# Mixed order in the last group of the attention sums, and four low parts of the first weights on GpSimd

## The chip, the cores and the metric

The kernel runs on one core of a Trainium2 chip. The metric is the device time of one execution in microseconds. Before the change the median of three runs was 1007.03 us (1006.68 to 1008.79).

## What is computed

Four graph layers over 1250 nodes with 1024 features, each with a layer norm and a relu ahead of it and added to its input:

```python
h = jnp.maximum(_layernorm(x), 0.0)
x = x + _L0_gnn_ref(h, ...)   # x1 = h @ W1 + b1 (512 columns), then four gated sums over a fixed graph
h = jnp.maximum(_layernorm(x), 0.0)
x = x + _L1_gnn_ref(h, ...)   # h @ W.T + bias, W scattered from the edges and their weights
h = jnp.maximum(_layernorm(x), 0.0)
x = x + _L2_gnn_ref(h, ...)   # graph convolution
h = jnp.maximum(_layernorm(x), 0.0)
x = x + _L3_gnn_ref(h, ...)   # graph attention

# inside _L3_gnn_ref
e = jnp.exp(-jax.nn.leaky_relu(al[src] + ar[dst], negative_slope=NEG_SLOPE))
rowsum = jax.ops.segment_sum(e, src, num_segments=N)
h_prime = jax.ops.segment_sum(e[:, None] * h[dst], src, num_segments=N)
return jax.nn.elu(h_prime / (rowsum[:, None] + EPS))
```

Two places matter here: the product with `W1` at the very start, and the weighted sums `h_prime` at the very end.

## The kernel before

The nodes lie in T = 10 tiles of 128 rows. Every float32 matrix product is made of three passes with the split of a value into a high part (rounded to the type that TensorE takes) and a low part (what is left): high by high, high by low, low by high. ScalarE writes the high parts with a copy, VectorE the low parts with a subtraction. All engines' programs are written out by hand and run in their written order; semaphores tie them together.

**The start.** `w1_raw` comes in four DMAs as KT = 8 pieces of 128x512. ScalarE writes `w1_hi[k]` (L1015) and counts `w_hi_ready`; VectorE writes `w1_lo[k]` = `w1_raw[k]` - `w1_hi[k]` for all eight (L1400) and counts `w_lo_ready`. Then VectorE goes on with the statistics of the third tile (L495 to L499), the choice of each window's edges (`here` L1297, `edges` L1300), `hT_lo` of the second tile (L553), the names of the cells (`src_i` L1305, `node` L1306 and on), and after more of the same the first groups of cells (`right` and `left`, L1340 to L1352), which TensorE sums (L1812, L1815) from its third tile on. TensorE's product of a tile (`x1_pe`, L1885 to L1887) takes three matmuls per piece; in the first tile each piece waits for `w_lo_ready`:

```python
if t == 0:
    pe.wait_ge(w_lo_ready, k + 1)
```

TensorE also transposes each next tile (L563), which ScalarE copies as `hT_hi` (L546). GpSimd's queue at that time: constants, the parts of the edge weights (L829 to L837, done by 14 us), then the storing of count rows (L841). Dense layers 1 and 3 count on with the same `w_lo_ready` in `product_pe`.

**The end.** The attention sums go over GROUPS = 5 groups of GRP = 2 tiles of nodes. A step s of a group takes the attention values between tile s and the group's 256 nodes: VectorE (L1672 to L1683), ScalarE (L1204, L1209) and GpSimd (`e_part`, L929) make `att_hi[s]` and `att_lo[s]`, and TensorE (`gat_step`, L2042) adds three products per tile j and half n of the 1024 columns into PSUM: six matmuls per tile j. `row_sums(j)` (L2049) then sums the attention values and counts `gat_ready`; ScalarE reads sums and row sums (L1218, L1219) and counts `gat_read`; VectorE and ScalarE finish the tile (L1692 to L1708, L1224, L1225), and SP stores it. In the first four groups TensorE takes both tiles j at each step. The last group is written out apart: all ten steps for tile 0, its row sums, ten steps for tile 1's first half, its row sums, ten steps for tile 1's second half:

```python
pe.wait_ge(gat_read, T - GRP - 1)
for s in range(T):
    pe.wait_ge(att_lo_ready, T * (GROUPS - 1) + s + 1)
    gat_step(s, 0, range(2))
row_sums(0).then_inc(gat_ready, 1)
pe.wait_ge(gat_read, T - GRP)
for s in range(T):
    gat_step(s, 1, [0])
row_sums(1).then_inc(gat_ready, 1)
for s in range(T):
    last = gat_step(s, 1, [1])
```

Of the kernel before, what the change touches and what calls it, by code (L numbers as in the profile page):

```python
# [14 lines left out]
ALU = mybir.AluOpType  # L15
ACT = mybir.ActivationFunctionType
AX_X = mybir.AxisListType.X
F32 = mybir.dt.float32
# [12 lines left out]
T = -(-N // P)  # L31
NP = T * P
KT = D // P
# [23 lines left out]
GRP = 2  # L57
# [2 lines left out]
SLOTS = 5  # L60
TANH_LEAD = 3
AL_FIRST = T - 2
LAST_SUMS = (2, 3, 4, 0, 1)
EARLY = 3
LN_STEPS = 3
NORM_STEPS = 4
EPS_LN = 1e-5
# [6 lines left out]
def build_program(nc, x, src, dst, edge_weight, w1, b1, gate_w, gate_b, bias1, w2, b2, w3, att, out):  # L74
# [22 lines left out]
    def sem(name):  # L97
        return ctx.enter_context(nc.semaphore(name))
# [20 lines left out]
    w1_raw = at("w1_raw", [P, KT, HID], F32, R_Y + 64 * KIB)  # L119
    w1_hi = at("w1_hi", [P, KT, HID], F32R, R_Y + 24 * KIB)  # L120
# [171 lines left out]
    w_landed = sems("w_landed", 4)  # L292
    w_hi_ready = sem("w_hi_ready")
    w_lo_ready = sem("w_lo_ready")
    copy_landed = sem("copy_landed")
    first_stored = sem("first_stored")
    bias_placed = sem("bias_placed")
# [178 lines left out]
    def split_act(act, d, ks):  # L476

        for k in ks:
            if k % 2 == 0:
                act.wait_ge(w_landed[k // 2], 16 * (d.n + 1))  # L480
            nc.scalar.activation(W_HI[d.n][:, k, :], W_RAW[d.n][:, k, :], ACT.Copy).then_inc(w_hi_ready, 1)

    def split_dve(dve, d, ks):

        for k in ks:
            dve.wait_ge(w_hi_ready, KT * d.n + k + 1)
            nc.vector.tensor_tensor(W_LO[d.n][:, k, :], W_RAW[d.n][:, k, :], W_HI[d.n][:, k, :].bitcast(F32),
                                    ALU.subtract).then_inc(w_lo_ready, 1)
# [77 lines left out]
    def product_pe(pe, d, i, b, first, transpose_next):  # L566

        t = 2 * i + b
        hi, lo = W_HI[d.n], W_LO[d.n]
        pe.wait_ge(hT_lo_ready, d.tiles(t + 1))  # L570
        pe.wait_ge(product_read[b], d.pairs(i))
        for k in range(KT):
            if k == KT // 2 and transpose_next is not None:
                transpose_next()
            if first:
                pe.wait_ge(w_lo_ready, KT * d.n + k + 1)
            for left, rights in ((hT_hi[b], (hi, lo)), (hT_lo[b], (hi,))):
                for half in range(2):
                    for right in rights:
                        last = nc.tensor.matmul(PRODUCT[d.n][b][:, half * BANK:(half + 1) * BANK], left[:, k, :],  # L580
                                                right[:, k, half * BANK:(half + 1) * BANK],
                                                start=(k == 0 and left is hT_hi[b] and right is hi),
                                                stop=(k == KT - 1 and left is hT_lo[b]))
        last.then_inc(product_ready[b], 1)
# [218 lines left out]
    def _(pool):  # L803
# [31 lines left out]
        nc.gpsimd.tensor_tensor(left_over[1], left_over[0], part[1], ALU.subtract).then_inc(parts_chain, 1)  # L835
        pool.wait_ge(parts_chain, 4)
        nc.gpsimd.tensor_copy(part[2], left_over[1]).then_inc(parts_chain, 1)  # L837

        for a in range(T):
            pool.wait_ge(count_row_ready, a + 1)  # L840
# [31 lines left out]
        d = dense[1]  # L872
# [397 lines left out]
    def _(dve):  # L1270
# [124 lines left out]
        pick_rows()  # L1395
        transposed_dve(dve, d0, 0, 0)
        scale_dve(dve, d0, 0)
        for k in range(KT):
            dve.wait_ge(w_hi_ready, k + 1)
            nc.vector.tensor_tensor(w1_lo[:, k, :], w1_raw[:, k, :], w1_hi[:, k, :].bitcast(F32),  # L1400
                                    ALU.subtract).then_inc(w_lo_ready, 1)
# [359 lines left out]
    def _(pe):  # L1761
# [102 lines left out]
        def x1_pe(t):  # L1864

            b = t % 2
            pe.wait_ge(hT_lo_ready, t + 1)
            if t == 1:
                pe.wait_ge(blend_chain, 3)
                open_bank(1)  # L1870
            if t + 1 < T:
                transpose_pe(pe, d0, (t + 1) // 2, (t + 1) % 2)
            for k in range(KT):
                if k % 2 == 0:
                    place_pe(t, k // 2)
                if k == 0:
                    pe.wait_ge(bias_placed, t + 1)
                if t == 1 and k == KT // 2:
                    sum_captured()
                if t == T - 1 and k == 2:  # L1880
                    pe.wait_ge(product_read[0], HT)
                    spread_u(0, 0)
                if t == 0:
                    pe.wait_ge(w_lo_ready, k + 1)
                nc.tensor.matmul(PRODUCT0[b], hT_hi[b][:, k, :], w1_hi[:, k, :], start=False, stop=False, skip_group_check=True)  # L1885
                nc.tensor.matmul(PRODUCT0[b], hT_hi[b][:, k, :], w1_lo[:, k, :], start=False, stop=False, skip_group_check=True)  # L1886
                last = nc.tensor.matmul(PRODUCT0[b], hT_lo[b][:, k, :], w1_hi[:, k, :], start=False, stop=(k == KT - 1), skip_group_check=True)  # L1887
            last.then_inc(product_ready[b], 1)
# [158 lines left out]
        def row_sums(j):  # L2047

            return nc.tensor.matmul(DEN[j], e_sum[:, j * P:(j + 1) * P], ones[:, 0:2], start=True, stop=True)  # L2049
# [20 lines left out]
        with pe.Fori(1, GROUPS - 1) as grp:  # L2070
            gat_pe(grp, False)

        pe.wait_ge(gat_read, T - GRP - 1)
        for s in range(T):
            pe.wait_ge(att_lo_ready, T * (GROUPS - 1) + s + 1)
            gat_step(s, 0, range(2))
        row_sums(0).then_inc(gat_ready, 1)
        pe.wait_ge(gat_read, T - GRP)
        for s in range(T):
            gat_step(s, 1, [0])  # L2080
        row_sums(1).then_inc(gat_ready, 1)
        for s in range(T):
# [25 lines left out]
```

## Time and profile before

| | us |
|---|---|
| median of the runs | 1007.03 |
| the profiled execution | 1009.05 |
| its span, first to last instruction | 1007.5 |
| TensorE busy | 982.6 (98%) |
| VectorE busy | 672.2 (67%) |
| ScalarE busy | 430.4 (43%) |
| GpSimd busy | 126.1 (13%) |

The mean granted clock of TensorE is 0.996 of full speed. TensorE is busy nearly all the time; of the span, 24.9 us are left in which it isn't. A few microseconds are shown best by its waits and by the timelines of the first 50 us and of the last 45.

### The profile page before, as it was taken

How to read it: one execution, taken by the hardware profiler on the slowest of the kernel's cores; microseconds unless marked ns; L12 is line 12 of the kernel's file. 1: busy time of each engine (PE TensorE's matmuls, PEld its weight loads, DVE VectorE, ACT ScalarE, POOL GpSimd, SP SyncE). 2: the span in 40 equal slices, each digit the busy share in tenths (PEclk: the TensorE clock that was granted, in tenths of full speed). 3: DMA queues.
4: the chain of work that ended last, by engine and by line, in shares of the span. 5: the costliest groups of instructions: out<-in, count | busy, mean ns of one | idle time of the engine just before them, and what ended most of it. 6: DMA issues, size and time to landing. Idle time of an engine off the chain costs nothing.

```text
span 1007.5 us, 14740 instructions
## 1 busy us (share of the span) xinstructions
PE 982.6 (98%) x5170; PEld 811.6 (81%) x5170; DVE 672.2 (67%) x1251; ACT 430.4 (43%) x655; POOL 126.1 (13%) x160
## 2 busy tenths in 40 slices
PE   6899999999999999999999999999999999999987
PEld 4688888888888888888888888888888888888865
DVE  7888889788777978444494343127356556988883
ACT  5688865554543655221142222242223233354452
POOL 2011400000000010232221000001100000333330
PEclk9999999999999999999999999999999999999998
DMA  7256580000000013755533111322442120111113
GB/s 249 89 182 224 131 258 1 1 22 0 0 21 0 0 23 92 178 202 177 181 108 105 42 42 42 146 105 104 167 153 83 68 99 0 44 65 71 52 70 113
DMA packets 27326, 93.42 MB, mean 93 GB/s; under 512 B 3530, under 2 KB 3530, under 8 KB 27136
## 3 DMA queue, kind: packets, MB, share of 16 engines
q1 hardware_dynamic: 16400, 58.07, 16.6%
q0 software_dynamic: 10880, 34.74, 11.3%
q8 instruction: 29, 0.48, 0.2%
q14 instruction: 17, 0.14, 0.1%
HBM read 64.48 MB, written 33.56 MB: 97 GB/s over the span
## 4 chain that ended last, share of the span: by engine, by line
PE 89%; DVE 8%; issue 2%; ACT 1%; DMA 0%; ACTq 0%; DVEq 0%
PE ps L580 32%; PE ps L2042 12%; PE ps L1962 9%; PE ps L1964 9%; PE ps L1963 9%; PE ps L2015 5%; PE ps L2014 5%; PE ps L563 3%; PE ps L1885 1%; PE ps L1887 1%; PE ps L1886 1%; PE ps L1856 1%; PE ps L1812 1%; PE ps L1815 1%; DVE left L1345 1%
## 5 line engine op out<-in xcount | busy, mean ns | idle before, releaser
L1962 PE MATMUL ps<-g_hi,mask_hi 128*128 128x512 f32 x400 | 157.4, 393 | 1.2 <-DVE mask_lo L1503 1.2
L1964 PE MATMUL ps<-g_hi,mask_lo 128*128 128x512 f32 x400 | 155.8, 390 | 0.0
L1963 PE MATMUL ps<-g_lo,mask_hi 128*128 128x512 f32 x400 | 155.7, 389 | 0.0
L580 PE MATMUL ps<-w_hi,hT_hi 128*128 128x512 f32 x320 | 126.4, 395 | 0.0
L546 ACT ACTIVATE hT_hi<-ps 128x1024 fp32r<-128x1024 f32 x40 | 41.0, 1026 | 198.6 <-PE ps L563 198.6
L580 PE MATMUL ps<-w_lo,hT_hi 128*128 128x512 f32 x320 | 124.7, 390 | 0.0
L2042 PE MATMUL ps<-y_all,att_hi 128*128 128x512 f32 x400 | 112.0, 398 | 4.6 <-DVE att_lo L1683 4.6
L1098 ACT ACTIVATE mask<-ps,v 128x640 f32<-128x640 f32 x80 | 63.5, 794 | 111.7 <-PE ps L1964 52.8
L580 PE MATMUL ps<-w_hi,hT_lo 128*128 128x512 f32 x320 | 98.7, 389 | 0.0
L2042 PEld LDWEIGHTS ps<-y_all,att_hi 128*128 128x128 f32 x400 | 74.8, 191 | 22.3 <-DVE att_lo L1683 6.8
L1962 PEld LDWEIGHTS ps<-g_hi,mask_hi 128*128 128x128 f32 x400 | 75.1, 188 | 19.6 <-DVE mask_lo L1503 3.3
L1964 PEld LDWEIGHTS ps<-g_hi,mask_lo 128*128 128x128 f32 x400 | 75.1, 188 | 15.8
L1963 PEld LDWEIGHTS ps<-g_lo,mask_hi 128*128 128x128 f32 x400 | 75.1, 188 | 15.2
L553 DVE TENSOR_TENSOR hT_lo<-ps,hT_hi 128x1024 fp32r<-128x1024 f32 x40 | 48.9, 1222 | 45.5 <-ACT hT_hi L546 45.5
L1498 DVE TENSOR_TENSOR mask<-mask,countT 128x640 f32<-128x640 f32 x80 | 65.5, 819 | 14.4 <-ACT mask L1098 14.4
L580 PEld LDWEIGHTS ps<-w_hi,hT_lo 128*128 128x128 f32 x320 | 60.1, 188 | 12.8
L580 PEld LDWEIGHTS ps<-w_lo,hT_hi 128*128 128x128 f32 x320 | 60.1, 188 | 11.9
L580 PEld LDWEIGHTS ps<-w_hi,hT_hi 128*128 128x128 f32 x320 | 60.1, 188 | 11.8
L1503 DVE TENSOR_TENSOR mask_lo<-mask,mask_hi 128x640 fp32r<-128x640 f32 x80 | 65.4, 818 | 0.6 <-ACT mask_hi L1103 0.6
L1103 ACT ACTIVATE mask_hi<-mask 128x640 fp32r<-128x640 f32 x80 | 58.8, 735 | 15.3 <-DVE mask L1498 15.0
L2042 PE MATMUL ps<-y_all,att_lo 128*128 128x512 f32 x200 | 64.4, 395 | 0.0
L580 PE MATMUL ps<-wt_hi,hT_hi 128*128 128x512 f32 x160 | 63.3, 396 | 0.0
(197 smaller groups left out, 1831.2 us busy)
## 6 DMA issues: line engine op xcount, KB each, us to landing
xin<-x_after SPq DMA_DIRECT2D x30, 512.0 KB, 3.3
xres<-x_after POOLq DMA_DIRECT2D x20, 512.0 KB, 4.1
x_after<-xres POOLq DMA_DIRECT2D x20, 512.0 KB, 3.0
w_raw<-in_L_gnn_W SPq DMA_DIRECT2D x8, 1024.0 KB, 7.6
x_after<-g POOLq DMA_DIRECT2D x20, 256.0 KB, 7.1
xres<-x_after SPq DMA_DIRECT2D x10, 512.0 KB, 3.3
xin<-in_x SPq DMA_DIRECT2D x9, 512.0 KB, 3.4
out_x<-xres SPq DMA_DIRECT2D x9, 512.0 KB, 2.6
```

The source lines that it names most:

```text
L553: nc.vector.tensor_tensor(hT_lo[b][:, :, :].rearrange("p k m -> p (k m)"), TRANSPOSED, hT_hi[b][:, :, :].rearrange("p k m -> p (k m)").bit ...
L580: last = nc.tensor.matmul(PRODUCT[d.n][b][:, half * BANK:(half + 1) * BANK], left[:, k, :], right[:, k, half * BANK:(half + 1) * BANK], st ...
L1098: nc.scalar.activation(mask[k][:, :], U_ALL, ACT.Tanh, bias=v[:, s:s + 1]).then_inc(tanh_ready, 1)
L1103: nc.scalar.activation(mask_hi[k][:, :], mask[k][:, :], ACT.Copy).then_inc(mask_hi_ready, 1)
L1498: nc.vector.tensor_tensor(mask[k][:, :], mask[k][:, :], countT[:, s, h * HALF:(h + 1) * HALF], ALU.mult).then_inc(mask_ready, 1)
L1503: nc.vector.tensor_tensor(mask_lo[k][:, :], mask[k][:, :], mask_hi[k][:, :].bitcast(F32), ALU.subtract).then_inc(mask_lo_ready, 1)
L1962: nc.tensor.matmul(SUMS[dd], mask_hi[k][:, cols], g_hi[:, s, :], start=(s == 0), stop=False)
L1963: nc.tensor.matmul(SUMS[dd], mask_hi[k][:, cols], g_lo[:, s, :], start=False, stop=False)
L1964: last = nc.tensor.matmul(SUMS[dd], mask_lo[k][:, cols], g_hi[:, s, :], start=False, stop=(s == T - 1))
L2014: nc.tensor.matmul(out_n, left, y_hi[s][:, n * BANK:(n + 1) * BANK], start=(s == 0), stop=False)
L2015: last = nc.tensor.matmul(out_n, left, y_lo[s][:, n * BANK:(n + 1) * BANK], start=False, stop=(s == T - 1))
L2042: last = nc.tensor.matmul(AGG[j][:, n * BANK:(n + 1) * BANK], left, right[:, n * BANK:(n + 1) * BANK], start=(s == 0 and len(rights) == 2 ...
```

## The change

Two independent edits.

1. In the last group of the attention sums, steps 0 to 6 add tile 1's first half right after tile 0 (nine matmuls a step); the last TAIL = 3 steps of that half follow after `row_sums(0)`, and then `row_sums(1)` and the second half as before. The waits for `gat_read` stand inside step 0.
2. GpSimd writes `w1_lo` for the last POOL_LOWS = 4 pieces, with a semaphore of its own, `w1_lo_pool`; VectorE writes the first four. The count of `w_lo_ready` for the later layers is four lower (`lows_before`).

```diff
--- before.py
+++ after.py
@@ -60,8 +60,10 @@
 SLOTS = 5
 TANH_LEAD = 3
 AL_FIRST = T - 2
+POOL_LOWS = 4
 LAST_SUMS = (2, 3, 4, 0, 1)
 EARLY = 3
+TAIL = 3
 LN_STEPS = 3
 NORM_STEPS = 4
 EPS_LN = 1e-5
@@ -292,6 +294,7 @@
     w_landed = sems("w_landed", 4)
     w_hi_ready = sem("w_hi_ready")
     w_lo_ready = sem("w_lo_ready")
+    w1_lo_pool = sem("w1_lo_pool")
     copy_landed = sem("copy_landed")
     first_stored = sem("first_stored")
     bias_placed = sem("bias_placed")
@@ -480,6 +483,9 @@
                 act.wait_ge(w_landed[k // 2], 16 * (d.n + 1))
             nc.scalar.activation(W_HI[d.n][:, k, :], W_RAW[d.n][:, k, :], ACT.Copy).then_inc(w_hi_ready, 1)
 
+    def lows_before(d):
+        return KT * d.n - POOL_LOWS
+
     def split_dve(dve, d, ks):
 
         for k in ks:
@@ -573,7 +579,7 @@
             if k == KT // 2 and transpose_next is not None:
                 transpose_next()
             if first:
-                pe.wait_ge(w_lo_ready, KT * d.n + k + 1)
+                pe.wait_ge(w_lo_ready, lows_before(d) + k + 1)
             for left, rights in ((hT_hi[b], (hi, lo)), (hT_lo[b], (hi,))):
                 for half in range(2):
                     for right in rights:
@@ -835,6 +841,10 @@
         nc.gpsimd.tensor_tensor(left_over[1], left_over[0], part[1], ALU.subtract).then_inc(parts_chain, 1)
         pool.wait_ge(parts_chain, 4)
         nc.gpsimd.tensor_copy(part[2], left_over[1]).then_inc(parts_chain, 1)
+        for k in range(KT - POOL_LOWS, KT):
+            pool.wait_ge(w_hi_ready, k + 1)
+            nc.gpsimd.tensor_tensor(w1_lo[:, k, :], w1_raw[:, k, :], w1_hi[:, k, :].bitcast(F32),
+                                    ALU.subtract).then_inc(w1_lo_pool, 1)
 
         for a in range(T):
             pool.wait_ge(count_row_ready, a + 1)
@@ -1395,7 +1405,7 @@
         pick_rows()
         transposed_dve(dve, d0, 0, 0)
         scale_dve(dve, d0, 0)
-        for k in range(KT):
+        for k in range(KT - POOL_LOWS):
             dve.wait_ge(w_hi_ready, k + 1)
             nc.vector.tensor_tensor(w1_lo[:, k, :], w1_raw[:, k, :], w1_hi[:, k, :].bitcast(F32),
                                     ALU.subtract).then_inc(w_lo_ready, 1)
@@ -1881,7 +1891,10 @@
                     pe.wait_ge(product_read[0], HT)
                     spread_u(0, 0)
                 if t == 0:
-                    pe.wait_ge(w_lo_ready, k + 1)
+                    if k < KT - POOL_LOWS:
+                        pe.wait_ge(w_lo_ready, k + 1)
+                    else:
+                        pe.wait_ge(w1_lo_pool, k - (KT - POOL_LOWS) + 1)
                 nc.tensor.matmul(PRODUCT0[b], hT_hi[b][:, k, :], w1_hi[:, k, :], start=False, stop=False, skip_group_check=True)
                 nc.tensor.matmul(PRODUCT0[b], hT_hi[b][:, k, :], w1_lo[:, k, :], start=False, stop=False, skip_group_check=True)
                 last = nc.tensor.matmul(PRODUCT0[b], hT_lo[b][:, k, :], w1_hi[:, k, :], start=False, stop=(k == KT - 1), skip_group_check=True)
@@ -2070,13 +2083,17 @@
         with pe.Fori(1, GROUPS - 1) as grp:
             gat_pe(grp, False)
 
-        pe.wait_ge(gat_read, T - GRP - 1)
         for s in range(T):
             pe.wait_ge(att_lo_ready, T * (GROUPS - 1) + s + 1)
+            if s == 0:
+                pe.wait_ge(gat_read, T - GRP - 1)
             gat_step(s, 0, range(2))
+            if s == 0:
+                pe.wait_ge(gat_read, T - GRP)
+            if s < T - TAIL:
+                gat_step(s, 1, [0])
         row_sums(0).then_inc(gat_ready, 1)
-        pe.wait_ge(gat_read, T - GRP)
-        for s in range(T):
+        for s in range(T - TAIL, T):
             gat_step(s, 1, [0])
         row_sums(1).then_inc(gat_ready, 1)
         for s in range(T):
```

TensorE at the start of the last group, before (`ps` is PSUM; `att_hi_121` to `_130` and `att_lo_111` to `_120` are steps 0 to 9; x4 is two halves by two right sides):

```order
L2042 MATMUL ps<-y_all,att_hi_121 128x512 x4
L2042 MATMUL ps<-y_all,att_lo_111 128x512 x2
L2042 MATMUL ps<-y_all,att_hi_122 128x512 x4
L2042 MATMUL ps<-y_all,att_lo_112 128x512 x2
L2042 MATMUL ps<-y_all,att_hi_123 128x512 x4
```

and changed:

```order
L2055 MATMUL ps<-y_all,att_hi_121 128x512 x4
L2055 MATMUL ps<-y_all,att_lo_111 128x512 x2
L2055 MATMUL ps<-y_all,att_hi_121 128x512 x2
L2055 MATMUL ps<-y_all,att_lo_111 128x512
L2055 MATMUL ps<-y_all,att_hi_122 128x512 x4
L2055 MATMUL ps<-y_all,att_lo_112 128x512 x2
```

Step 0 now has three matmuls more, those of tile 1's first half, ahead of step 1. So have steps 1 to 6.

TensorE around the first row sums of that group, before:

```order
L2042 MATMUL ps<-y_all,att_hi_129 128x512 x4
L2042 MATMUL ps<-y_all,att_lo_119 128x512 x2
L2042 MATMUL ps<-y_all,att_hi_130 128x512 x4
L2042 MATMUL ps<-y_all,att_lo_120 128x512 x2
L2049 MATMUL ps<-ones,e_sum 128x2
L2042 MATMUL ps<-y_all,att_hi_121 128x512 x2
L2042 MATMUL ps<-y_all,att_lo_111 128x512
```

and changed:

```order
L2055 MATMUL ps<-y_all,att_hi_129 128x512 x4
L2055 MATMUL ps<-y_all,att_lo_119 128x512 x2
L2055 MATMUL ps<-y_all,att_hi_130 128x512 x4
L2055 MATMUL ps<-y_all,att_lo_120 128x512 x2
L2062 MATMUL ps<-ones,e_sum 128x2
L2055 MATMUL ps<-y_all,att_hi_128 128x512 x2
L2055 MATMUL ps<-y_all,att_lo_118 128x512
L2055 MATMUL ps<-y_all,att_hi_129 128x512 x2
L2055 MATMUL ps<-y_all,att_lo_119 128x512
L2055 MATMUL ps<-y_all,att_hi_130 128x512 x2
L2055 MATMUL ps<-y_all,att_lo_120 128x512
L2062 MATMUL ps<-ones,e_sum 128x2
```

Between the two row sums stand nine matmuls where thirty stood; the other twenty-one moved ahead of them.

GpSimd after the parts of the edge weights, before:

```order
L835 TENSOR_TENSOR ew_rest<-ew_rest,ew_part 80x250
L837 CAST ew_part<-ew_rest 80x250
L841 DMA count_rows<-count_row_192 128x1280
L844 DMA weight_rows<-weight_row_194 128x1024
L841 DMA count_rows<-count_row_193 128x1280
```

and changed:

```order
L841 TENSOR_TENSOR ew_rest<-ew_rest,ew_part 80x250
L843 CAST ew_part<-ew_rest 80x250
L846 TENSOR_TENSOR w_lo<-w_raw,w_hi 128x512 x4
L851 DMA count_rows<-count_row_192 128x1280
L854 DMA weight_rows<-weight_row_194 128x1024
```

The four subtractions stand between the casts and the first stores; VectorE's row of the same form, x8 before, is x4.

## Rows read from the trace of the kernel before

**Rows 1.** The waits of TensorE: us in total, times, the longest.

```profile
PE ps L1812 <- DVE right L1352: 5.0, 3, 2.5
PE ps L2042 <- DVE att_lo L1683: 4.6, 6, 1.8
```

**Rows 2.** Timeline of TensorE, last group: start, duration, instruction, [idle before, releaser].

```profile
966.22 1.17 PE L2042 MATMUL ps<-y_all,att_hi 128*128 128x512 f32 x4
...
967.68 1.07 PE L2042 MATMUL ps<-y_all,att_hi 128*128 128x512 f32 x4
...
971.76 1.07 PE L2042 MATMUL ps<-y_all,att_hi 128*128 128x512 f32 x4
...
974.25 1.20 PE L2042 MATMUL ps<-y_all,att_hi 128*128 128x512 f32 x4 [0.97 <-DVE att_lo L1683]
...
978.02 1.20 PE L2042 MATMUL ps<-y_all,att_hi 128*128 128x512 f32 x4 [0.15 <-DVE att_lo L1683]
...
981.51 1.20 PE L2042 MATMUL ps<-y_all,att_hi 128*128 128x512 f32 x4 [1.83 <-DVE att_lo L1683]
...
984.65 2.07 PE L2042 MATMUL ps<-y_all,att_hi 128*128 128x512 f32 x4 [1.09 <-DVE att_lo L1683]
...
995.54 0.71 PE L2042 MATMUL ps<-y_all,att_hi 128*128 128x512 f32 x2
```

**Rows 3.** Two windows: length, busy (x count) PE PEld DVE ACT POOL, PEclk, DMA, GB/s.

```profile
40.00:44.00 4.00, 2.01 (x24) 1.43 (x21) 3.82 (x8) 2.38 (x4) 0.00 (x0) 1.00 0.00 0
983.00:989.00 6.00, 4.91 (x13) 3.56 (x12) 1.91 (x4) 1.09 (x2) 0.18 (x1) 0.50 0.56 183
```

**Rows 4.** Timelines of ScalarE and VectorE, last group and end.

```profile
966.46 1.02 ACT L1219 ACTIVATE gat_sums<-ps 128x1024 f32<-128x1024 f32 x1
...
987.83 0.17 ACT L1218 ACTIVATE rden<-ps 128x1 f32<-128x1 f32 x1 [6.26 <-PE ps L2049]
...
995.71 0.17 ACT L1218 ACTIVATE rden<-ps 128x1 f32<-128x1 f32 x1 [3.80 <-PE ps L2049]
...
1002.64 0.69 ACT L1265 ACTIVATE elu_neg<-ps,rden 128x512 f32<-128x512 f32 x1 [4.40 <-PE ps L2042]
...
992.23 1.23 DVE L1708 TENSOR_TENSOR xres<-elu_neg,gat_sums 128x1024 f32<-128x1024 f32 x1
...
998.46 0.69 DVE L1708 TENSOR_TENSOR xres<-elu_neg,gat_sums 128x512 f32<-128x512 f32 x1
```

**Rows 5.** Timeline of TensorE, first product and first cells.

```profile
23.70 0.39 PE L1885 MATMUL ps<-w_hi,hT_hi 128*128 128x512 f32 x1
...
31.79 1.06 PE L563 MATMUL ps<-ident,xin 128*128 128x128 f32 x8 [0.25 <-ACT xin L539]
34.63 0.21 PE L1812 MATMUL ps<-right,left 125*128 125x90 bf16 x1 [1.78 <-DVE right L1352]
```

**Rows 6.** Timelines of VectorE and ScalarE, first weights.

```profile
15.80 3.70 DVE L1400 TENSOR_TENSOR w_lo<-w_raw,w_hi 128x512 fp32r<-128x512 f32 x6 [0.19 <-ACT w_hi L1015]
...
22.27 1.21 DVE L553 TENSOR_TENSOR hT_lo<-ps,hT_hi 128x1024 fp32r<-128x1024 f32 x1
...
23.59 0.41 DVE L1306 TENSOR_TENSOR node<-edges,firsts 125x250 f32<-125x250 f32 x1
...
15.15 3.21 ACT L1015 ACTIVATE w_hi<-w_raw 128x512 fp32r<-128x512 f32 x6
...
19.57 1.05 ACT L546 ACTIVATE hT_hi<-ps 128x1024 fp32r<-128x1024 f32 x1
```

**Rows 7.** Timelines of GpSimd and VectorE where both work.

```profile
962.14 0.74 POOL L929 TENSOR_TENSOR e_part<-e_part,att_e 128x256 f32<-128x256 f32 x1 [0.90 <-DVE att_e L1678]
...
426.49 2.38 POOL L880 TENSOR_TENSOR xres<-xres,row_all 128x1024 f32<-128x1024 f32 x1 [6.27 <-DVE xres L1587]
...
428.48 1.22 DVE L553 TENSOR_TENSOR hT_lo<-ps,hT_hi 128x1024 fp32r<-128x1024 f32 x1 [0.44 <-ACT hT_hi L546]
...
505.22 2.38 DVE L514 TENSOR_TENSOR square<-rough 128x2 f32<-128x2 f32 x1
```

## The prediction

> **What bounds the kernel now.** The page has TensorE busy nearly all the time, so the end can move only by its idle stretches or by a stretch at the lower clock. I read its waits next: 5.0 us in three for VectorE's `right` (the cells), and 4.6 us in six for `att_lo` [rows 1]. The change touches one of each. TensorE's timeline in the last group of the attention sums and the granted clock there give the price of the second [rows 2, 3]; the timelines of the first 35 us give that of the first [rows 5, 6].
>
> **The last group, before.** TensorE starts it at 966.22 and does six matmuls a step: 1.46 us for the first step (967.68 - 966.22), then 1.36 each ((971.76 - 967.68) / 3), or 0.227 a matmul [rows 2]. VectorE makes `att_lo` more slowly than that, so TensorE waits: step 8 starts at 981.51 and step 9 at 984.65, each right after its `att_lo`, with 1.83 and 1.09 us idle; most of the 4.6 us lies in this group. The waits cost the clock too: it is 0.50 (1.2 GHz) from 983 to 989 [rows 3], so that step 9's four `att_hi` matmuls take 2.07 us. After step 9 no input is new: two passes of 30 matmuls follow, the last from 995.54 until ScalarE starts on it at 1002.64, 7.10 us [rows 2, 4].
>
> **The last group, after.** The same 120 matmuls, nine instead of six in each of the first seven steps. VectorE's times don't move: nothing that it waits for in this group comes from TensorE's work of this group.
> (1) Step 0: six matmuls, to 967.68, then the wait for `gat_read`. ScalarE has read the second pair of banks at 966.46 + 1.02 = 967.48 [rows 4], so it costs nothing; behind it on TensorE stand only matmuls, and nobody waits for those three. They end at 968.36.
> (2) Steps 1 to 6: 6 x 9 x 0.2275 = 12.3 us, to 980.65. Step 5 is asked for at 976.55 and step 6 at 978.6. In the old order step 5 had its `att_lo` at 974.25, and step 7 started at 978.02 after 0.15 idle [rows 2], so step 6, six matmuls before that, had its own by 976.6. No wait.
> (3) Steps 7 and 8: 12 x 0.227 = 2.7 us, to 983.4; step 8's `att_lo` is there at 981.5.
> (4) Step 9 can't start before 984.65: one idle stretch of 1.3 us is left.
> (5) Six matmuls, 1.38 us, to 986.03; row sums 0.14; nine matmuls 2.05, to 988.2; row sums 0.14, to 988.36.
> (6) The last pass, 7.10 us: ScalarE's last step starts at 995.46 instead of 1002.64, **7.2 us earlier**.
> The clock is taken at its upper level throughout: in 40 to 44 us TensorE is busy 2.01 us of 4.00, with an idle stretch of 2.5 us after steady work, and the clock stays at 1.00 [rows 1, 3].
>
> **Is what follows still hidden?** ScalarE and VectorE work on the first row sums' tile from 987.83 to 992.23 + 1.23 = 993.46, 5.6 us, and on the second's from 995.71 to 998.46 + 0.69 = 999.15, 3.4 us [rows 4]. Now the first starts at 986.34 (986.03 and 0.31 for the row sums, as at the second ones) and ends at 992.0; the second follows on the same engines, done by 995.4. One short VectorE piece comes after it; VectorE is next wanted 0.8 us after 995.46, ScalarE at 995.46. It fits, by about half a microsecond. What follows the last matmul is unchanged.
>
> **The first weights.** VectorE is rid of four of eight `w_lo`. Six take 3.70 us from 15.80 [rows 6], 0.617 each: the fourth is done at 17.03, the eighth was at 19.50. What lies between them and `hT_lo` of the second tile takes 22.27 - 19.50 = 2.8 us, so VectorE comes to `hT_lo` by 20.0 or a little later, and there ScalarE's `hT_hi` is ready at 19.57 + 1.05 = 20.62 [rows 6]. It starts at 20.66 instead of 22.27: 1.6 us, not 2.5.
> GpSimd: `w_hi` of piece 4 is the third of six ScalarE copies from 15.15, done near 16.8 [rows 6]. A GpSimd tensor_tensor takes 0.74 us for 256 columns and 2.38 for 1024 [rows 7]; by the line through both, 512 take 1.29, and the two rows are the bounds. The fourth `w_lo` on VectorE holds the first piece until 17.05; the four end at 18.3, 19.7, 21.0 and 22.3. TensorE comes to piece 7 at 23.70 [rows 5] and to piece 4 nine matmuls of 0.228 earlier, 21.65: hidden, by 1.4 us at the tightest. GpSimd's next queue entry, the storing of the first count rows, waits for work that comes after 45 us.
>
> One part is taken back. A VectorE tensor_tensor of 128x2 that began with a GpSimd add at 505.2 took 2.38 us, as long as the add; one that reads PSUM, at 428.48 inside an add, took its usual 1.22 [rows 7]. VectorE's `node` has both operands in SBUF and would start at 23.59 - 1.61 = 21.98 [rows 6], inside the last GpSimd piece: 0.3 us lost, and 1.3 us are left. The Trainium skill (SBUF — State Buffer, "SBUF: two separate sides") speaks against the change here: VectorE and GpSimd share a port pair as an exclusive lock, and a VectorE instruction with two SBUF inputs stands still while a GpSimd one that reads SBUF has it. By that rule this part is worth 1.3 us, without it 1.6; the 2.38 us row agrees with the rule.
>
> Does TensorE get it? Its transposes of the fourth tile begin at 31.79, of which 0.25 is their own wait for ScalarE (which comes earlier too), and end near 32.6; it then stands until 34.63 for the first cells [rows 5]. VectorE has no gap from there to the next wait of 2.5 us, so TensorE resumes 1.3 us earlier at both. At most it could be 34.63 - 32.6 = 2.0 us, at least nothing. No later wait of TensorE is for anything with a time of its own, so the 1.3 us reach the end.
>
> **Sum.** 7.2 + 1.3 = 8.5 us. The profiled execution took 1009.05 us (span 1007.5) and would take 1000.5; it lies 2.0 above the median of the runs, 1007.03. Against the median: **998.5 us**. A measurement of this kernel tells about 0.2% (2 us) from no change.
>
> **The rivals.**
> *The clock still falls (0.08).* The 1.3 us before step 9 may be enough. For it: the old fall came with TensorE waiting in this place. Against: then it had idled before several steps in a row, steps 5, 7 and 8 among them [rows 2], now it has worked steadily for 15 us, and 2.5 us before 44.5 did not do it [rows 1, 3]. Price: six microseconds at half speed, 3 us [rows 3]: 1001.5. The Trainium skill (TensorE: Matmul & The Clock Gate, "Why this matters for your kernels") lists idle gaps between bursts of matmuls as what brings the lower clock back; no row here shows where between 2.5 us once and the old pattern the limit lies.
> *The early part gives nothing (0.08).* GpSimd meets VectorE more than counted, or takes nearer 2.38 us a piece: the last is done near 26.6, 3 us after TensorE wants it, and the 2.0 us before the first cells are used up. Time 999.8 to 1001.
> *The tail shows (0.08).* The two chains of ScalarE and VectorE, now back to back, or the stores behind them on SP's queue, end after the last matmul. The margin is 0.5 us; the excess I put at up to 1.5, somewhat less than the 2.2 us that used to lie between the chains (995.71 - 993.46): 999 to 1000.
> *Slower (0.01, and 0.01 for no change).* GpSimd's pieces hold TensorE in its first product. Slower by 0.2% needs 7.2 + 2.0 of slack + 2.0 = 11.2 us, the last piece at 34.9, or 4.5 us a piece against 1.29; from 3.9 a piece on, the gain is gone. For it: GpSimd and VectorE do block each other [rows 7]. Against: VectorE has nothing with two SBUF operands between 17.05 and 21.98.
>
> **How the numbers follow.** Forecast 0.74, the three rivals of the same sign 0.08 each, the last 0.02. Range: below, an early part of 2.0 and the spread of the runs (their lowest is 0.35 under the median, their highest 1.8 over it) with room for a lower run, 996.3; above, the fallen clock, 1001.6. Faster 0.97, within 0.2% 0.02, slower 0.01.
>
> **What would show it.** TensorE should have one wait for `att_lo` in the last group, of 1.2 to 1.4 us, and a granted clock of 1.00 to the end. GpSimd should show four pieces of 1.2 to 1.4 us that end before 22.6, with no wait of TensorE for them, `hT_lo` near 20.7, a stretched `node`, and TensorE's wait for the first cells 0.5 to 0.8 us long. A second idle stretch near 981, a clock of 0.50 after 985, or a VectorE piece of the first two chains that ends after the last matmul would make it wrong.

## The result and the profile after

| us | before | after |
|---|---|---|
| median of the runs | 1007.17 (1006.68 to 1008.79, 5 runs) | 1002.55 (1001.09 to 1002.92, 5 runs) |
| the profiled execution | 1009.05 | 1002.79 |
| its span | 1007.5 | 1001.3 |
| TensorE busy | 982.6 | 979.9 |
| VectorE busy | 672.2 | 667.6 |
| GpSimd busy | 126.1 | 130.8 |

By the medians the kernel is faster by 4.6 us, where 8.5 were forecast. The ratio on record, here and below, is 0.9945, with its 95% interval [0.9932, 0.9958]. It lies near the ratio of the means, not that of the medians (0.9954), and so counts single long runs of before too: it stands for 5.5 us (4.2 to 6.9), and leaves 8.5 out as well. The median of 1002.55 lies above the forecast range, whose upper end was 1001.6. The spans of the two profiled executions differ by 6.2 us, more than the medians do; part of the answer lies in that difference.

**The end.** The waits of TensorE after the change, with their totals, times and longest (compare [rows 1]):

```profile
PE ps L1822 <- DVE right L1362: 4.6, 3, 2.5
...
PE ps L2055 <- DVE att_lo L1693: 1.5, 2, 1.1
```

Of 4.6 us for `att_lo` 1.5 are left. TensorE's timeline of the last group shows how, and answers to [rows 2]:

```profile
966.86 1.17 PE L2055 MATMUL ps<-y_all,att_hi 128*128 128x512 f32 x4
...
968.33 0.63 PE L2055 MATMUL ps<-y_all,att_hi 128*128 128x512 f32 x2
...
981.29 1.07 PE L2055 MATMUL ps<-y_all,att_hi 128*128 128x512 f32 x4
...
982.65 1.07 PE L2055 MATMUL ps<-y_all,att_hi 128*128 128x512 f32 x4
...
985.31 1.20 PE L2055 MATMUL ps<-y_all,att_hi 128*128 128x512 f32 x4 [1.14 <-DVE att_lo L1693]
...
986.81 0.28 PE L2062 MATMUL ps<-ones,e_sum 128*128 128x2 f32 x2
...
989.12 0.28 PE L2062 MATMUL ps<-ones,e_sum 128*128 128x2 f32 x2
989.25 0.71 PE L2055 MATMUL ps<-y_all,att_hi 128*128 128x512 f32 x2
```

Steps 0 to 8 have no bracket: they run without a wait. One idle stretch of 1.14 us stands before step 9. The windows around it (columns as in [rows 3]; the clock is the last figure but two) and the last pieces of the finishing chains on ScalarE and VectorE (compare [rows 4]):

```profile
984.00:986.00 2.00, 0.86 (x4) 0.60 (x4) 1.26 (x2) 0.00 (x0) 0.00 (x0) 1.00 0.14 39
986.00:990.00 4.00, 4.00 (x21) 3.33 (x20) 1.07 (x3) 1.99 (x3) 0.00 (x0) 1.00 0.70 243
```

```profile
996.38 0.69 ACT L1275 ACTIVATE elu_neg<-ps,rden 128x512 f32<-128x512 f32 x1 [1.57 <-PE ps L2055]
...
995.64 0.42 DVE L1761 TENSOR_SCALAR xres<-xres 128x512 f32<-128x512 f32 x1
997.17 0.69 DVE L1764 SCALAR_TENSOR_TENSOR elu_neg<-elu_neg,xres 128x512 f32<-128x512 f32 x1 [1.11 <-ACT elu_neg L1275]
```

The granted clock stays at 1.00. VectorE is through with the two chains at 995.64 + 0.42 = 996.06, 1.1 us before it is wanted again. From the group's first matmul to ScalarE's last step pass 996.38 - 966.86 = 29.52 us, where the prediction's steps had 995.46 - 966.22 = 29.24 and the profile of before 36.42. So the profiles show 6.9 us gained here. But the group starts at 966.86, 0.64 us *later* than before: 6.9 - 0.64 is the 6.2 between the spans. The gain of the first weights has not reached this place.

**The start.** VectorE and GpSimd at the first weights (compare [rows 6]):

```profile
15.87 1.29 DVE L1410 TENSOR_TENSOR w_lo<-w_raw,w_hi 128x512 fp32r<-128x512 f32 x2 [0.19 <-ACT w_hi L1025]
18.47 1.29 DVE L501 BATCH_NORM_STATS2 stats<-xin 128x6 f32<-128x512 f32 x2 [1.31 <-DMA xin<-in_x]
...
21.33 1.21 DVE L559 TENSOR_TENSOR hT_lo<-ps,hT_hi 128x1024 fp32r<-128x1024 f32 x1
...
22.65 0.41 DVE L1316 TENSOR_TENSOR node<-edges,firsts 125x250 f32<-125x250 f32 x1
```

```profile
16.95 5.11 POOL L846 TENSOR_TENSOR w_lo<-w_raw,w_hi 128x512 fp32r<-128x512 f32 x4 [3.63 <-ACT w_hi L1025]
```

GpSimd does as forecast: 5.11 / 4 = 1.28 us a piece, done at 22.06, and no wait of TensorE names it. VectorE is free of `w_lo` at 17.16 and then stands 1.31 us for a **DMA**: the third tile of `x`, whose statistics come next, has not landed. With the weights' loads under way such a load takes 8.7 us from issue to landing (the median of the two issued in 3 to 20 us, against 3.3 over the whole page). Before, four more `w_lo` covered that landing. `hT_lo` starts at 21.33, not at 20.66. TensorE has the first cells, and later the fourth group's, here (compare [rows 5]):

```profile
33.69 0.21 PE L1822 MATMUL ps<-right,left 125*128 125x90 bf16 x1 [1.37 <-DVE right L1362]
...
43.58 0.20 PE L1822 MATMUL ps<-right,left 125*128 125x90 bf16 x1 [2.51 <-DVE right L1362]
...
44.89 1.95 PE L1838 MATMUL ps<-ident,weights_sd 128*128 128x128 f32 x8
...
48.29 1.03 PE L569 MATMUL ps<-ident,xin 128*128 128x128 f32 x8
```

The first cells come 34.63 - 33.69 = 0.94 us earlier, and so does the end of the 2.5 us stand (44.53 before). Then it turns round: the eight transposes at 44.89 take 1.95 us, where the profile of before has 1.07. The windows say why:

```profile
40.00:43.50 3.50, 1.07 (x5) 0.56 (x3) 3.32 (x8) 2.76 (x4) 0.00 (x0) 1.00 0.00 0
43.50:47.00 3.50, 3.42 (x39) 3.42 (x40) 3.50 (x8) 1.27 (x3) 0.00 (x0) 0.54 0.02 5
```

The granted clock fell behind the stand (the stretch in which TensorE stands idle), to 0.54. The next tile's transposes start at 48.29, where before they stood at 47.76: 0.94 gained, 1.47 lost. The same stretches in the profile of before, on the other hand, have the clock at 1.00:

```profile
43.50:47.00 3.50, 2.47 (x41) 2.42 (x42) 3.50 (x8) 2.24 (x5) 0.00 (x0) 1.00 0.02 5
```

**Whose stand is it?** The wait is booked to VectorE's `right`, as all cells' matmuls wait for it. But the cells of that group were written at 38.13 + 0.77 = 38.90, 4.7 us before TensorE went on. What came last is on ScalarE's timeline, its copy of the third group's sums, whose PSUM the fourth group needs:

```profile
40.67 1.15 ACT L545 ACTIVATE xin<-xin,shift 128x1024 f32<-128x1024 f32 x1 [2.30 <-DVE shift L505]
41.73 0.67 ACT L1001 ACTIVATE ps<-b_all,bias_scale 128x512 f32<-128x512 f32 x1
42.34 0.71 ACT L965 ACTIVATE countT<-ps 128x500 int16<-128x500 f32 x1
42.92 0.52 ACT L965 ACTIVATE weights_sd<-ps 128x400 f32<-128x400 f32 x1
```

It ends at 43.44, and TensorE's stand at 43.58. ScalarE had nothing to do for 2.30 us, then took the relu of the fifth tile (L545), for which it had waited for VectorE's statistics, and only then this copy.

### The profile page after: what moved, and what is told of

Its sections match the earlier page's. It is cut to its first block, busy times and chain, and to the rows that moved or that the text cites. A ratio compares the mean times of both kernels' runs of the same rounds, so it can differ in the third digit from the quotient of the medians.

```text
span 1001.3 us, 14740 instructions
## 1 busy us (share of the span) xinstructions
PE 979.9 (98%) x5170; PEld 811.6 (81%) x5170; DVE 667.6 (67%) x1247; ACT 430.2 (43%) x655; POOL 130.8 (13%) x164
## 4 chain that ended last, share of the span: by engine, by line
PE 87%; DVE 9%; issue 2%; ACT 1%; DMA 1%; SPq 1%; ACTq 0%; DVEq 0%
PE ps L586 32%; PE ps L2055 11%; PE ps L1975 8%; PE ps L1977 8%; PE ps L1976 8%; PE ps L2028 5%; PE ps L2027 5%; PE ps L569 3%; PE ps L1898 1%; PE ps L1900 1%; PE ps L1899 1%; DVE wt_lo L493 1%; PE ps L1866 1%; DMA xin<-in_x 1%; PE ps L1822 1%
```

## The experiments

Three causes were put up for the missing 4 us. The sum was made against one execution in which the clock had fallen in the last group, which it may not do in every execution, and it may fall elsewhere. The lows give less than counted, by the DMA or by a lock between GpSimd and VectorE. And the stand near 44 us hangs on ScalarE's order, not on VectorE's cells. Every kernel below computes all of the reference. The sets were timed on three chips whose before has medians within 0.3 us of each other (1006.95 to 1007.25).

### The kernel of before, unchanged

No edit.

> The unchanged kernel, profiled a second time. Theory 1 (the profile of before was not typical: it lay 1.9 us over the median): the new profile has a shorter span than 1007.5, and what is missing lies in the last group of the attention sums, where the stretch at the lower clock (983 to 989 in the first profile) is shorter or absent. Theory 2 (the clock falls there in every execution, the scatter is elsewhere): again a granted clock of 0.50 for about 6 us before 990, whatever the span. Time within 0.1% of before.

Measured: 1007.67 us (1006.74 to 1009.10, 11 runs) against 1007.25 (1006.59 to 1010.97, 21 runs), 1.0001 [0.9992, 1.0010]. Its windows at the stand and around step 9, and TensorE at the group's first step and at step 9, with ScalarE's last step:

```profile
43.50:47.00 3.50, 2.47 (x35) 2.50 (x36) 3.50 (x8) 1.74 (x4) 0.00 (x0) 0.57 0.02 5
...
980.00:985.00 5.00, 2.52 (x10) 1.42 (x8) 4.93 (x6) 0.42 (x1) 2.51 (x2) 1.00 0.26 105
985.00:990.00 5.00, 4.16 (x19) 3.49 (x20) 1.86 (x5) 1.46 (x3) 0.00 (x0) 1.00 0.62 210
```

```profile
967.40 1.17 PE L2042 MATMUL ps<-y_all,att_hi 128*128 128x512 f32 x4
...
985.84 1.20 PE L2042 MATMUL ps<-y_all,att_hi 128*128 128x512 f32 x4 [1.49 <-DVE att_lo L1683]
...
1001.63 0.69 ACT L1265 ACTIVATE elu_neg<-ps,rden 128x512 f32<-128x512 f32 x1 [4.40 <-PE ps L2042]
```

With nearly the same waits and the same instructions, the clock held in the last group and step 9's four matmuls took 1.20 us, not 2.07. Group start to ScalarE's last step was 1001.63 - 967.40 = 34.23 us, not 36.42: the fall there cost 2.2 us, and not every execution has it. The times say the same: of the 21 runs of before, 12 lie at 1006.6 to 1007.5 us, eight at 1008.3 to 1009.3 and one at 1011.0, and the two profiled executions, each with a fall that cost time, took 1009.05 and 1008.02. So the median is most likely that of an execution without such a cost. In this second profiled execution the fall came at the 44 us stand instead, which the profile of before had passed at 1.00, and cost 1.2 us there (the next tile's transposes at 48.96, not 47.76). Against an execution whose clock holds in the last group, the mixed order is worth 34.23 - 29.52 = 4.7 us.

### The mixed order alone

```diff
-        for k in range(KT - POOL_LOWS, KT):
-            pool.wait_ge(w_hi_ready, k + 1)
-            nc.gpsimd.tensor_tensor(w1_lo[:, k, :], ...)
-        for k in range(KT - POOL_LOWS):
+        for k in range(KT):
```

> The mixed order of the last group alone; all eight low parts stay on VectorE. The two profiles give 6.9 us for this part (29.5 us from the group's first matmul to ScalarE's last step, against 36.4). Theory 1 (the profile of before was not typical): the median falls by 4.5 to 5.5 us, to about 1002.2. Theory 2 (it was typical, and the first part cost what is missing): it falls by 6.5 to 7 us, to about 1000.4.

Measured: 1002.31 us (1002.05 to 1002.62, 5 runs), 0.9944 [0.9931, 0.9958]: 4.9 us by the medians, the 4.7 of the traces and not 7.2. By the ratio it is 5.6 us (4.2 to 7.0), since the runs of before in which the clock fell weigh in it; 7.2 lies outside that too. That alone equals the whole change within the intervals, which are wide enough to hide one microsecond. Its profile has the 2.51 us stand as well, and the clock stays at 1.00 behind it.

### The four low parts alone

```diff
-            if s < T - TAIL:
-                gat_step(s, 1, [0])
...
-        for s in range(T - TAIL, T):
+        for s in range(T):
```

> The four low parts on GpSimd alone; the last group as before. Theory A (the loss in the first 50 us comes with the change: TensorE's stand before the fourth group of cells now ends in a fall of the clock): 0.9 us gained at the first cells, 1.4 lost after 43 us, so 0.5 us slower than before in most executions, and a granted clock near 0.5 between 43.5 and 47. Theory B (the fall is chance, and before has it as often): the median 0.9 us under before's.

Measured: 1006.95 us (1005.57 to 1009.44, 11 runs), 0.9991 [0.9980, 1.0003]: 0.3 us by the medians and 0.9 by the ratio, not told from none; the 0.5 us slower of theory A lies just outside the interval. The lowest runs differ by 1.0 us. In its profile VectorE waits 1.54 us for the same DMA, the first cells come at 33.91 (0.7 earlier), and the clock falls twice, before the stand (0.76 in 33 to 40 us) and in 980 to 985 (0.66). The fall before the stand cost nothing: TensorE was merely later at it, waited 1.11 us instead of 2.52, and went on at 43.82, still 0.71 us ahead of before. The fall in the last group cost next to nothing too. It came in 980 to 985 us, where before's had come in 983 to 989, and TensorE was back at 1.00 for the last two passes. From group start to ScalarE's last step pass 999.96 - 965.50 = 34.46 us, 0.2 more than with no fall: the slowed step 8 went into the wait before step 9, 0.40 us instead of 1.49. The scatter of the falls, 3.9 us from lowest to highest run here, hides a gain of one microsecond.

### ScalarE's copy ahead of the relu

In the changed kernel ScalarE takes the sums of the third group before it waits for the fifth tile's statistics:

```diff
+            if t == FIRST_STEP:
+                place_act(t, 2)
...
-            place_act(t, 2)
+            if t != FIRST_STEP:
+                place_act(t, 2)
```

> The changed kernel, and ScalarE's copy of the third group's cells (take_cells of group 2) put ahead of the relu of the fifth tile, which waits for VectorE. In the trace TensorE stands 2.5 us until 43.58 although the fourth group's cells were made by 38.9; ScalarE's copy of the third group ends at 43.44. Theory S (ScalarE's copy is what TensorE waits for): that wait falls under 0.5 us, the clock stays at 1.00 there, and the time is 3 to 4 us under the changed kernel's, about 999. Theory V (VectorE's cells, as the page names them): the wait stays 2.5 us, and the time is that of the changed kernel, 1002.5.

Measured: 999.88 us (999.80 to 1000.32, 5 runs), 0.9922 [0.9909, 0.9936]; it beats both kernels. The windows of the old stand, and ScalarE:

```profile
40.00:43.50 3.50, 3.50 (x46) 3.00 (x46) 3.32 (x7) 3.50 (x7) 0.00 (x0) 1.00 0.02 5
43.50:47.00 3.50, 3.50 (x54) 3.26 (x53) 3.50 (x8) 2.64 (x5) 0.00 (x0) 1.00 0.21 53
```

```profile
39.70 0.75 ACT L965 ACTIVATE countT<-ps 128x500 int16<-128x500 f32 x1 [1.27 <-PE ps L1828]
40.30 0.54 ACT L965 ACTIVATE weights_sd<-ps 128x400 f32<-128x400 f32 x1
40.73 1.15 ACT L545 ACTIVATE xin<-xin,shift 128x1024 f32<-128x1024 f32 x1
```

The stand is gone and TensorE busy throughout, though no cell of VectorE's comes earlier (the first at 33.74 us, 33.69 before this edit): the profile's name for that wait was wrong. The copies fit into ScalarE's idle time, and its relu starts at 40.73 instead of 40.67. At 44.20 instead of 48.29 us TensorE is at the next tile; of these 4.1 us, 1.5 of which are the other profile's fall of the clock, it gives back 1.2 at a new wait, `count_b` at 56 us, and is 2.9 ahead at 107 us. With no stand there is no fall of the clock there either: the five runs lie within 0.5 us, and none of the five profiles of kernels with this edit has a granted clock below 1.00 before 990 us.

### The changed kernel once more

> The changed kernel once more. Theory C (the fall of the clock at the stand before the fourth group of cells is chance, from execution to execution, and explains the scatter): times again between 1001.0 and 1003.0, the low end where it does not fall, about 1.4 us apart; the new profile may show it at 43.6 or not, and its span goes with that. Theory D (the fall belongs to the changed kernel): it is there again, and no time is under 1002.

Measured: 1001.89 us (1000.78 to 1002.93, 5 runs), 0.9944 [0.9930, 0.9957]. In this profiled execution the clock fell in 33 to 40 us, and the stand shrank:

```profile
33.00:40.00 7.00, 5.55 (x69) 4.57 (x70) 7.00 (x12) 3.51 (x6) 0.00 (x0) 0.76 0.47 150
40.00:43.50 3.50, 3.33 (x41) 2.39 (x39) 3.32 (x7) 2.69 (x5) 0.00 (x0) 1.00 0.00 0
43.50:47.00 3.50, 2.65 (x42) 2.55 (x43) 3.50 (x8) 2.24 (x5) 0.00 (x0) 1.00 0.02 5
```

Theory D is out: three of the five runs lie under 1002, and the clock did not fall behind the stand here. The same program has a span 0.9 us shorter, by where the clock fell. Its DMA wait was 2.22 us, so the first cells came at 34.45, hardly earlier than before: the start scatters with that landing too.

### The eight low parts back on VectorE

The kernel with the earlier copy, less the four pieces on GpSimd.

> The mixed order and the earlier ScalarE copy, with all eight low parts on VectorE: against taken_first it has the first weights' part of the change undone, with no stand left at which the clock could fall. Theory 1 (that part is worth what the DMA of the third tile leaves of it, about 0.9 us): 0.9 us over taken_first's 999.9, at 1000.8. Theory 2 (it is worth the 1.3 us of the forecast): 1001.2. Theory 3 (worth nothing): 999.9. The scatter of the runs stays near 0.5 us.

Measured: 1000.92 us (1000.73 to 1001.60, 5 runs), 0.9935 [0.9921, 0.9948], against 999.88 with them. Once the stand and its falls of the clock no longer cover it, edit 2 shows its worth: 1.04 us, where the forecast had 1.3. The runs of the two sets don't overlap (999.80 to 1000.32 and 1000.73 to 1001.60), but they are from two chips, whose medians of before differ by 0.2 us, so the 1.04 is no surer than that. Without the four pieces the earlier copy gains 1.4 us (from 1002.31), with them 2.0 or 2.7, by which of the changed kernel's two sets of runs one takes.

### The copies of x behind the tiles' loads

SP's copies of `x` go out one tile later and two loads of constants behind the fourth tile's load, so that the third tile's load meets less traffic (the moved loads of constants are left out below):

```diff
-            sp.dma_start(x1_dram[(t - 2) * P:(t - 1) * P, :], x[(t - 2) * P:(t - 1) * P, :]).then_inc(copy_landed, 16)
+            if t > 2:
+                sp.dma_start(x1_dram[(t - 3) * P:(t - 2) * P, :], x[(t - 3) * P:(t - 2) * P, :]).then_inc(copy_landed, 16)
...
```

> taken_first, with SP's copy of each x tile to memory put behind the next tile's load, and the loads of gate_b and gate_w moved behind that of the fifth tile: 1 MB less in the DMA queues ahead of the third tile. Theory M (VectorE, rid of four low parts, waits for the third tile's load, which shares the DMA engines with those): its stats start near 17.1 instead of 18.4, hT_lo of the second tile at 20.7 instead of 21.4, and the first cells 0.6 us earlier: 999.3. Theory N (the load is late for another reason): stats again at 18.4, 999.9.

Measured: 999.80 us (999.49 to 999.91, 5 runs), 0.9920 [0.9906, 0.9934]. VectorE's timeline:

```profile
16.97 1.28 DVE L501 BATCH_NORM_STATS2 stats<-xin 128x6 f32<-128x512 f32 x2
...
20.60 1.23 DVE L559 TENSOR_TENSOR hT_lo<-ps,hT_hi 128x1024 fp32r<-128x1024 f32 x1 [0.49 <-ACT hT_hi L552]
21.74 0.37 DVE L1321 CAST src_i<-edges 125x250 int32<-125x250 f32 x1
22.03 0.41 DVE L1322 TENSOR_TENSOR node<-edges,firsts 125x250 f32<-125x250 f32 x1
```

The third tile's load took 7.2 us, not 8.7. No wait for a DMA is left, and `hT_lo` starts at 20.60 behind ScalarE's `hT_hi`, where the forecast had 20.66: the load was the cause, the lock was not. `src_i` takes 0.37 us instead of the 0.28 of the changed kernel, and GpSimd works until 21.97 (16.85 + 5.12): 0.1 us, the only thing in this stretch that looks like a lock. `node` is not stretched, and it starts at 22.03, when GpSimd is done. The first cells come 0.68 us earlier than with the kernel above (33.06 against 33.74), and the median gains 0.1. The lead is still 0.67 us at 94.58 and only 0.08 at 95.70: between the eighth and the ninth of ten `count_b` transposes TensorE stands 0.44 us, and that is booked to no semaphore ("issue"). What it waited for is open.

### Two steps behind the first row sums, and one

Both on the kernel with the earlier copy: TAIL = 2, then TAIL = 1.

> taken_first with TAIL = 2: step 7 too takes nine matmuls, so 0.7 us of work moves into the wait for step 9's att_lo. If that wait is pure idle time (theory I): it falls from 1.1 to 0.45 us and the end comes 0.7 us earlier, 999.2, with VectorE's one-input piece still done before it is wanted again. If the chain of ScalarE and VectorE behind the row sums now sets the end (theory K): the last matmul comes 0.7 earlier and the time stays at 999.9.

Measured: 999.00 us (998.77 to 999.42, 5 runs), 0.9914 [0.9901, 0.9928], 0.9 below TAIL = 3. The wait before step 9 is 0.59 us.

> The same as with the last two steps of tile 1's first half behind the first row sums (999.00 us), with only the last one there. Theory G (the idle stretch before step 9 is the whole of the reserve): in that kernel step 9 still waits 0.59 us at 982.04. Three more matmuls before it (0.68 us) fill it, step 9 starts at 982.13 without a wait, and the last pass ends 0.6 us earlier: 998.4. Theory H (the finishing chains come out from behind the matmuls): the first row sums stay where they are, so VectorE is done with the second tile's piece at 992.79 as before, and would be wanted at 993.18 - 0.59 = 992.59. It comes 0.2 us late, and only 0.4 us of the 0.6 is left: 998.6. The times of G and H lie too close for the medians, the trace tells them apart: by H VectorE's step on the last half starts right behind its 0.42 us piece, without an idle stretch.

Measured: 999.33 us (998.59 to 1000.51, 5 runs), 0.9923 [0.9909, 0.9936]. VectorE's end with TAIL = 2 and then with TAIL = 1:

```profile
992.37 0.42 DVE L1764 TENSOR_SCALAR xres<-xres 128x512 f32<-128x512 f32 x1
993.18 0.69 DVE L1767 SCALAR_TENSOR_TENSOR elu_neg<-elu_neg,xres 128x512 f32<-128x512 f32 x1 [0.39 <-ACT elu_neg L1278]
```

```profile
992.47 0.42 DVE L1764 TENSOR_SCALAR xres<-xres 128x512 f32<-128x512 f32 x1
992.92 0.69 DVE L1767 SCALAR_TENSOR_TENSOR elu_neg<-elu_neg,xres 128x512 f32<-128x512 f32 x1
```

With one step the bracket is gone: VectorE's last part starts behind its own 0.42 us piece and not behind ScalarE. The finishing chains have come out from behind the matmuls. The end of the span moves by 0.3 us, and the medians don't tell the two apart (999.00 and 999.33, the runs of both overlap). TAIL = 2 has the lowest median of all the kernels that ran, 999.00, 8.0 us below the 1007.04 of before on the same chip.

## Why the prediction was right or wrong

**The last group, steps (1) to (6): right.** Every step came as worked out: no wait to step 8, one idle stretch of 1.14 (1.3), clock at 1.00, 29.52 us in all (29.24). Both rivals of that part, the falling clock and the chains that show, did not occur. (The price of 3 us that the first one had for a fall was high: 2.2 and 0.2 were measured in the old order.) Step 9 started 18.45 us after the group's first matmul, where the forecast had 18.43; what lay behind it took 0.3 us more, since its six matmuls took 1.50 us instead of 1.38 and the row sums and nine matmuls after them 2.44 instead of 2.33. The chains kept 1.1 us of room, not 0.5, since ScalarE's last step came those 0.3 us later and the second chain took less than counted. That room is not fixed: in the profile of the mixed order alone VectorE waited 1.30 us inside the second chain for the load of its `xres`, and 0.54 us was left. The prediction had no load in these chains. That they would show next is true (TAIL = 1).

**Its price of 7.2 us: wrong, and the largest error.** The step that failed is the comparison of 995.46 with 1002.64. The 1002.64 held a fall of the clock that the text itself had priced, "step 9's four `att_hi` matmuls take 2.07 us", and ascribed to the waits ("The waits cost the clock too"). In a second execution of the same kernel nearly the same waits brought no fall, where [rows 3] have 0.50, and in a third of the old order (the four low parts alone) the fall cost 0.2 us. Without it the term is 4.7, and the mixed order alone measured 4.9. The sum's last step carried the error over: a gain read off an execution 2.0 us above the median was taken in full from the median. That the profiled execution lay 2.0 us above it was the sign that it held something that the median did not; the fall is 2.2.

**The first weights, 1.3 us: the mechanism right, the size 0.94 (1.04 by the medians), the reason for the reduction wrong.** GpSimd's price (1.29, measured 1.28), its start and its end held. "What lies between them and `hT_lo` of the second tile takes 22.27 - 19.50 = 2.8 us, so VectorE comes to `hT_lo` by 20.0" took it that all of that work was ready, and it begins with a tile that was still on its way. Nothing was subtracted for the load, and 0.3 us for a lock: but `node` ran after GpSimd's last piece, in this run (22.65 against 22.06) and with the earlier load (22.03 against 21.97). The rule of the Trainium skill (SBUF — State Buffer, "SBUF: two separate sides") that the two engines share a port pair as a lock was therefore not tested by `node`, and the 0.1 us of `src_i` is all that the first weights show for it. The last group shows more. In the profile of before, GpSimd and then VectorE:

```profile
981.55 1.63 POOL L933 TENSOR_TENSOR e_sum<-e_part,att_e 128x256 f32<-128x256 f32 x1 [1.85 <-DVE att_e L1678]
```

```profile
982.62 1.64 DVE L1708 TENSOR_TENSOR xres<-elu_neg,gat_sums 128x1024 f32<-128x1024 f32 x1
```

This sum of two SBUF inputs on VectorE takes 1.64 us when it begins inside GpSimd's piece, and 1.23 at 992.23 with GpSimd idle [rows 4]. The GpSimd piece, which began inside VectorE's step before, takes 1.63 us where others of its size take 0.74 [rows 7]. Step 9's `att_lo` comes right behind that sum, so this meeting holds it back by 0.4 us, an estimate from 1.64 - 1.23. It is the same after the change (1.65 and 1.22), and so no part of the error.

**"No later wait of TensorE is for anything with a time of its own": not enough at 44 us, in the executions where the clock falls there.** "VectorE has no gap from there to the next wait of 2.5 us" took the profile's name for that wait. The end of the stand did move with the work before it, since the relu at its head waits for VectorE's statistics, so the lead passed through, by 0.95 us; then the fall of the clock took 1.2 to 1.5 us back. And "the clock stays at 1.00" after that stand was luck: of four profiles with a stand of 2.5 us there, two have a fall behind it. The prediction used it as the proof that the clock holds through idle stretches; the conclusion came true in the last group, in all eight profiles of kernels with the mixed order, its proof did not.

So 8.5 became 4.6: 2.5 from the price of the last group (7.2 to 4.7), 0.3 from the first weights, and the rest, 1.1 (0.5 by the second set of runs), goes with the falls near 44 us, which take the start's gain back in part of the executions. That last share is inferred. For it: the lowest runs, 1006.59 before and 1000.78 after, are 5.8 us apart, close to 4.7 + 1.0, and half of the changed kernel's ten runs lie at 1002.5 or more, while those of the mixed order alone lie within 0.6 us. But two of these five have a mean granted clock of 0.997, against 0.999 in its profile, so they had a fall as well, which doesn't show in their times, and one or two profiles a kernel don't show how often each has which. Whether edit 2 makes the fall behind the stand more frequent is open: before has it too. The range failed by all of these together. The first alone would have given 998.5 + 2.5 = 1001.0, within it; no case in the range had before's clock holding without the change.

## What to carry to other kernels

When a profiled execution lies above the median of its runs, look for what it holds that the others don't, a fall of the clock first, and take its price out of the sum before a gain is read from it: a profile of the same kernel taken again shows whether it belongs to the kernel. Before work is taken off an engine, ask of each input of what follows when it lands: the removed work may have covered a load. And a wait on several semaphores is named in the profile by one of them; look at when that one was done, and if it was long before, find the engine whose last instruction ends at the end of the stand: here a copy that stood behind another wait, and moving it gave another 2.0 to 2.7 us on top of the change's 4.6 (1.4 without edit 2).

## What was not expected of the hardware

The granted clock of the same program differs between executions. Behind the stand of 2.5 us at 44 us it was 1.00 in one execution of before and in the mixed order alone, 0.57 in another of before, and 0.54 after the change; in the last group of before it was 0.50 in 983 to 989 us in one and 1.00 in the other. A fall cost 1.2 to 1.5 us at the first place and 2.2 at the second. It cost nothing where a stand followed that absorbed it (0.76 in 33 to 40 us), and 0.2 us in the last group where most of it lay ahead of a wait (0.50 in 982 to 984 us, the four low parts alone). So what a fall cost went by whether a wait followed it, and not by its length alone. The medians of one kernel moved with it, the changed kernel's by 0.7 us from one set of five runs to the next, while the kernels without the stand scattered by 0.4 to 0.9 us, one of them (TAIL = 1) by 1.9.

The third tile's load, which took 8.7 us in the changed kernel's first profile where the median of such loads is 3.3, landed at a time that varied: it took 9.1 and 9.6 us in two others, and VectorE's wait for it ran from 1.03 to 2.22 us over the six profiles with it.

In the attention sums of every kernel here GpSimd and VectorE lengthened each other: 1.64 us instead of 1.23 on VectorE, 1.63 and 1.79 instead of 0.74 on GpSimd.
